# Attention by head pairs on halves of the TensorE array in steps of 512 queries, with projections, norms and weight folding rearranged in front of it

## What is computed

```python
x = x + attn_a(layernorm(x))          # binding by FFT, done as matmuls; not touched by the change
x = x + ffn(layernorm(x))             # top 2 of 8 low-rank experts
x = x + attn_b(layernorm(x))
x = x + ffn(layernorm(x))
# attn_b(x), with x already normalised once; 16 heads of 64
x_norm = (x - mu) / sqrt(var + 1e-5) * ln_w + ln_b        # a norm of the norm
q = l2norm(split_heads(x_norm @ Wq)); k = l2norm(split_heads(x_norm @ Wk))
v = split_heads(x @ Wv)
align = einsum('bhtd,bhsd->bhts', q, k)
resonance = sigmoid((align - 0.29514) * 15.0)
modulation = resonance * gate_q[..., :, None] * gate_k[..., None, :]   # q.gq and k.gk, by head
out = einsum('bhts,bhsd->bhtd', modulation, v) @ Wo + bo
```

## Time and profile before

| | |
|---|---|
| time, median of 3 runs | 2682.93 us (2682.44 to 2709.91) |
| time of the profiled execution | 2679.45 us |
| its span (slowest core, core 6) | 2677.8 us; the others 2663.7 to 2677.1 |
| PE, DVE, ACT, POOL busy | 56%, 41%, 25%, 1% of the span |
| granted TensorE clock, mean | 0.716 of full speed |
| lnC | 713 to 857 us |
| queries and keys, values, key norms | 857 to 1451 us |
| attention with Wo | 1451 to 2456 us |
| last ffn with its norm | 2456 to 2678 us |

### The profile page before, as it was taken

How to read it: one execution, slowest core, us unless ns; L and a number is a source line. 1 busy time by engine, 2 the same in 40 slices (tenths; PEclk the granted TensorE clock), 3 DMA queues, 4 the chain that set the end, 5 groups by cost and what they waited for, 6 DMA issues and landing times.

```text
span 2677.8 us, 18415 instructions; the slowest of 8 cores (2663.7 to 2677.8 us)
## 1 busy us (share of the span) xinstructions
PE 1488.9 (56%) x5855; PEld 567.4 (21%) x5930; DVE 1102.0 (41%) x1281; ACT 677.0 (25%) x677; POOL 35.7 (1%) x57
## 2 busy tenths in 40 slices
PE   1699966232111535358222888788767888875141
PEld 1234422120000212223000222222212222222110
DVE  5422231452366565643997332232233333212532
ACT  0000000000000000000221777776257777650000
POOL 1000000100000000000000000000000000001000
PEclk9999978655555767679555777777967777778555
DMA  7020114724411113210100000000210000007224
GB/s 157 32 32 24 48 55 169 161 64 140 158 63 63 47 55 71 63 32 16 32 0 0 0 1 0 1 0 1 91 35 1 0 1 0 1 1 164 95 81 170
DMA packets 63794, 142.27 MB, mean 53 GB/s; under 512 B 23507, under 2 KB 25043, under 8 KB 63702
## 3 DMA queue, kind: packets, MB, share of 16 engines
q1 hardware_dynamic: 36870, 124.28, 14.1%
q0 software_dynamic: 26832, 16.82, 4.9%
HBM read 119.10 MB, written 37.75 MB: 59 GB/s over the span
## 4 chain that ended last, share of the span: by engine, by line
PE 44%; DVE 19%; DMA 13%; ACT 10%; issue 7%; DVEq 6%; SPq 1%; ACTq 0%; POOLq 0%
DMA xcb<-xb 9%; ACT fmA L1128 8%; PE pP L704 7%; PE pP L652 6%; DMA xcb<-x 4%; PE pA L391 3%; PE pB L391 3%; PE pP L686 3%; PE pA L686 3%; DVEq L778 3%; PE pB L686 3%; PE pA L568 3%; DVE xcb L834 2%; PE pB L568 2%; PE pP L373 2%
## 5 line engine op out<-in xcount | busy, mean ns | idle before, releaser
L373 PE MATMUL pP<-ident,scb 128*128 128x128 bf16 x512 | 64.7, 306 | 390.2 <-DVE scb L805 251.6
L1128 ACT ACTIVATE fmA<-pA,cpool 128x1024 bf16<-128x1024 f32 x172 | 208.5, 1212 | 84.3 <-PE pA L686 84.3
L1128 ACT ACTIVATE fmA<-pP,cpool 128x1024 bf16<-128x1024 f32 x170 | 206.0, 1212 | 83.9 <-PE pP L686 78.8
L1128 ACT ACTIVATE fmA<-pB,cpool 128x1024 bf16<-128x1024 f32 x170 | 206.0, 1212 | 78.8 <-PE pB L686 78.7
L704 PE MATMUL pP<-fmA,act 128*64 128x512 bf16 x512 | 185.2, 541 | 0.0
L1053 DVE COPY handle<-pP 64x1024 f32<-64x1024 f32 x32 | 39.1, 1222 | 351.1 <-PE pP L704 351.1
L652 PE MATMUL pP<-fmA,act 128*64 128x512 bf16 x512 | 170.8, 507 | 5.6 <-ACT fmA L1128 5.6
L686 PE MATMUL pA<-act,act 64*128 64x512 bf16 x344 | 124.0, 447 | 49.5 <-ACT fmA L1128 42.5
L686 PE MATMUL pP<-act,act 64*128 64x512 bf16 x340 | 123.3, 449 | 49.0 <-ACT fmA L1128 42.1
L686 PE MATMUL pB<-act,act 64*128 64x512 bf16 x340 | 123.0, 448 | 47.8 <-ACT fmA L1128 40.9
L373 PEld LDWEIGHTS pP<-ident,scb 128*128 128x128 bf16 x512 | 49.5, 138 | 406.2 <-issue 406.2
(11 more groups left out here) (194 smaller groups left out, 1843.5 us busy)
## 6 DMA issues: line engine op xcount, KB each, us to landing
xcb<-xb SPq DMA_DIRECT2D x128, 512.0 KB, 3.9
xb<-xcb SPq DMA_DIRECT2D x48, 512.0 KB, 2.9
xcb<-x SPq DMA_DIRECT2D x32, 512.0 KB, 4.2
y<-xcb SPq DMA_DIRECT2D x16, 512.0 KB, 2.9
skew<-handle SPq DMA_DIRECT2D x16, 256.0 KB, 2.2
Wb<-aWk POOLq DMA_DIRECT2D x1, 2048.0 KB, 21.7
Wb<-aWv POOLq DMA_DIRECT2D x1, 2048.0 KB, 39.8
Wb<-aWq POOLq DMA_DIRECT2D x1, 2048.0 KB, 17.5
```

The source lines that it names most:

```text
L373: mm = t.transpose(pTb[:, base + 128 * j:base + 128 * (j + 1)], scb1[:, 128 * j:128 * (j + 1)], ident[:])
L1128: s.activation(RB[:, 1024 * sc:1024 * (sc + 1)], (pA, pB, pP1)[RING_SLOT[pos]][:], AF.Sigmoid, bias=cpool[:, 0:1], scale=cpool[:, 1:2]).th ...
```

## The change

- One-pass norm of the norm. The variance of a normed row follows from that of the row, so lnC computes both factors from one bn_aggr (swu, rwu), applies one scale and shift from x to the cast tile sqb, and evicts the transposes on ACT. fmA then holds x_norm (without ln_w and ln_b) for keys, queries and values alike, and the values are multiplied by cfac when they leave PSUM. The 32 repeated loads, norms and transposes are gone.
- ln_w is folded into Wk and Wq: SP loads them in f32 by 16 pieces into xcb, alternating with the loads of x, and POOL multiplies each piece into Wb1 or Wb0 and casts an unscaled copy (wub), of which PE makes the row ln_b @ W. That row goes through DRAM into a column (qkb) that ACT adds as a bias. Wv is loaded into act3 early, Wo into Wb1 after the keys.
- Projections by 16 units u (keys, then queries) of 128 outputs x 2048 tokens, in 4 chunks of 512. ACT writes keys or queries and their squares. PE sums the squares of a chunk over each head onto 32 columns of the array (norm_sums; the four chunks on four column groups of one PSUM bank); DVE clamps; POOL raises the sums to the power -0.5, splits the result into a bf16 high part and a rest, and PE spreads both from 32 rows of the array (norm_spread); DVE multiplies. Key gates come out token-major (gate_k), and POOL multiplies them into the values (v_scale).
- Attention by pairs of heads: 32 blocks b of 512 queries (half, pair, half of that), 16 steps each. In a step PE computes the scores of both heads, head a on rows 64a to 64a+63 of the array and into its own bank of pA or pB, and then the sums over the key tile of two steps ago, head a on columns 64a to 64a+63, both into one bank of pP1. ACT takes one sigmoid of 128 x 1024 (512 queries of two heads) into a ring of four places in xcb2. The score ring has two PSUM tensors instead of three.
- Wo of the first 1024 tokens is spread over the steps of the second half, 9 matmuls a block at most one in a step; that of the last 1024 stays behind the loop.
- At the start five more POOL instructions and two small loads stand ahead of the weight loads, and PE and DVE wait for POOL's whole setup before the first norm.

The diff, cut to its core:

```diff
+    colT = fmA
+    RB = AP(xcb2.ap().tensor, 0, [[2048, 128], [1, 2048]]).bitcast(BF16)
...
+        fence(g.memset(E4[:], 0.0))
...
+        g.dma_start(out=lnwc[:], in_=AP(dram["blnw"], 0, [[1, 128], [128, DC]]),
...
+        g.wait_ge(wf.lb, 16)
...
+        for i in range(16):
+            dc = i % DC
+            wst = xcb[:, 1024 * (i % 2):1024 * (i % 2) + 1024]
+            dst = Wb1 if i < DC else Wb0
+            g.wait_ge((wf.ld0, wf.ld1)[i % 2], 16 * (i // 2 + 1))
+            g.tensor_scalar(dst[:, 1024 * dc:1024 * (dc + 1)], wst,
+                            lnwc[:, dc:dc + 1], None, ALU.mult).then_inc(wf.fold, 1)
+            if i >= 2:
+                g.wait_ge(wf.mm, i - 1)
+            g.tensor_copy(wub[:, 1024 * (i % 2):1024 * (i % 2) + 1024], wst
+                          ).then_inc(wf.copy, 1)
...
+        def v_scale(u):
+            g.wait_ge(pr.ge, u + 1)
...
+            g.tensor_tensor(vv, vv, gb, ALU.mult).then_inc(pr.vs, 1)
...
+        for u in range(16):
+            if u == 8:
+                g.wait_ge(pr.pj, 32)
+                wload(Wb1, "bWo", wl.bWo)
+                bload("bbo", wl.bbo)
+            g.wait_ge(pr.cl, u + 1)
+            g.tensor_tensor(ssb[:], ssb[:], AP(mhalf.ap().tensor, 0, [[1, 128], [0, 512]]),
+                            ALU.pow)
+            g.drain()
+            g.tensor_copy(hib[:], ssb[:])
+            g.drain()
+            g.tensor_scalar(tmb[:], hib[:], nlo[:, 0:1], None, ALU.mult)
+            g.drain()
+            if u >= 1:
+                g.wait_ge(pr.bc, 4 * u)
+            else:
+                g.wait_ge(su.ee, 2)
+            g.tensor_tensor(hlb[:], ssb[:], tmb[:], ALU.add).then_inc(pr.rs, 1)
+            if 1 <= u <= 8:
+                v_scale(u - 1)
...
+                y.wait_ge(wf.fold, i - 1)
+                y.wait_ge(wf.copy, i - 1)
+            else:
+                y.wait_ge(ffB.ost0, 128)
+                y.wait_ge(ffB.ost1, 128)
+            y.dma_start(out=xcb[:, 1024 * (i % 2):1024 * (i % 2) + 1024],
+                        in_=AP(dram["bWk" if i < DC else "bWq"], 128 * 1024 * (i % DC),
+                               [[1024, 128], [1, 1024]])
+                        ).then_inc((wf.ld0, wf.ld1)[i % 2], 16)
+        for q in range(2):
...
-        ln_transposes(lnC, (ffB.te, TC), [])
...
+            t.wait_ge(wf.copy, tc + 1)
...
+        def proj(u, c):
+            ec = u % DC
+            W_ = Wb1 if u < DC else Wb0
+            if c == 0 and ec == 0:
+                t.wait_ge(wf.fold, 8 if u < DC else 16)
+            if u >= 1:
+                t.wait_ge(pr.sq, 4 * (u - 1) + c + 1)
+            else:
+                t.wait_ge(bv.ev, TC)
+            ps = psab(c // 2)[:, 512 * (c % 2):512 * (c % 2) + 512]
+            for dc in range(DC):
+                mm = t.matmul(ps, W_[:, 1024 * dc + 128 * ec:1024 * dc + 128 * (ec + 1)],
+                              fmA[:, T * dc + 512 * c:T * dc + 512 * (c + 1)],
+                              start=(dc == 0), stop=(dc == DC - 1))
+            mm.then_inc(pr.pj, 1)
...
+        def norm_sums(u):
+            t.wait_ge(pr.sq, 4 * u + 4)
+            if u >= 1:
+                t.wait_ge(pr.cl, u)
+            else:
+                t.wait_ge(wf.row, 2)
+            for c in range(4):
+                mm = t.matmul(pP1[32 * c:32 * c + 32, 0:512], E4[:, 0:32],
+                              sqb[:, 2048 * (u % 2) + 512 * c:
+                                  2048 * (u % 2) + 512 * (c + 1)],
+                              start=True, stop=True)
+            mm.then_inc(pr.ss, 1)
...
+        def norm_spread(u):
+            t.wait_ge(pr.rs, u + 1)
+            for c in range(4):
+                k = 4 * u + c
                 if k >= 2:
...
+                    t.wait_ge(pr.nm, k - 1)
                 else:
                     t.wait_ge(lnC.ev, TC)
...
+                    t.wait_ge(su.ee, 2)
+                t.matmul(pP2[:, 512 * (c % 2):512 * (c % 2) + 512],
+                         Ebc[32 * c:32 * c + 32, :], hlb[32 * c:32 * c + 32, :],
+                         start=True, stop=True).then_inc(pr.bc, 1)
...
+        def gate_k(u):
...
+            for tc in range(TC):
+                mm = t.matmul(pP1[:, 512 + 2 * tc:512 + 2 * tc + 2],
+                              act3[:, T * u + 128 * tc:T * u + 128 * (tc + 1)],
+                              gk2[:, 0:2], start=True, stop=True)
+            mm.then_inc(pr.gm, 1)
...
+        for u in range(18):
+            if u < 16:
+                proj(u, 0)
+            if 1 <= u <= 16:
+                norm_sums(u - 1)
+            if u < 16:
+                proj(u, 1)
+            if 2 <= u < 10:
+                gate_k(u - 2)
+            if u < 16:
+                proj(u, 2)
+                proj(u, 3)
+            if 1 <= u <= 16:
+                norm_spread(u - 1)
...
+        def scores(i):
+            b, sc = i // TC, i % TC
+            th, hp, tb = b // 16, (b // 2) % HP, b % 2
+            ps = psab(i)
+            q0 = T * hp + 1024 * th + 512 * tb
+            for a in range(2):
+                mm = t.matmul(ps[:, 512 * a:512 * (a + 1)],
+                              act3[64 * a:64 * a + 64,
+                                   T * hp + 128 * sc:T * hp + 128 * (sc + 1)],
+                              act2[64 * a:64 * a + 64, q0:q0 + 512],
                               start=True, stop=True)
...
+            mm.then_inc(at.al, 1)
...
+        def key_sums(i):
+            b, sc = i // TC, i % TC
+            hp = (b // 2) % HP
+            if sc == 0 and b >= 2:
+                t.wait_ge(at.ev, b - 1)
+            for a in range(2):
+                mm = t.matmul(pP1[64 * a:64 * a + 64, 512 * (b % 2):512 * (b % 2) + 512],
+                              act1[:, 1024 * sc + 128 * hp + 64 * a:
+                                   1024 * sc + 128 * hp + 64 * (a + 1)],
+                              RB[:, 1024 * (i % 4) + 512 * a:
+                                 1024 * (i % 4) + 512 * (a + 1)],
+                              start=(sc == 0), stop=(sc == TC - 1))
+            mm.then_inc(at.av, 1)
...
+        def gate_q(b):
+            th, hp, tb = b // 16, (b // 2) % HP, b % 2
+            if b >= 1:
+                t.wait_ge(at.ge, b)
+            q0 = T * hp + 1024 * th + 512 * tb
+            t.matmul(pP2[:, 512:1024], gq2rep[:], act2[:, q0:q0 + 512],
+                     start=True, stop=True).then_inc(at.gm, 1)
...
+        for i in range(32 * TC + 2):
+            if i >= 2:
+                t.wait_ge(at.sg, i - 1)
+            if i < 32 * TC:
+                scores(i)
+            if i == 2:
+                t.wait_ge(pr.vs, HP)
+                t.wait_ge(pr.ge, HP)
+            if i >= 2:
+                key_sums(i - 2)
+            if i % TC == 8:
+                gate_q(i // TC)
+            f, j = i // TC - 16, i % TC - 4
+            if 0 <= f < 16 and 0 <= j <= HP:
+                if j == 0:
+                    if f == 0:
...
-    RING_SLOT, RING_FREE = [], {}
...
+                mm = wo_mm(f, j, pP2[:, 0:512])
+                if j == HP:
+                    mm.then_inc(wo.mm, 1)
...
+            v.tensor_scalar(sqb[:, 2048 * (tc % 2):2048 * (tc % 2) + 1024],
+                            xcb2[:, 1024 * (tc % 2):1024 * (tc % 2) + 1024],
+                            mv1[:, 2 * tc:2 * tc + 1], rwu[:, 2 * tc:2 * tc + 1],
+                            ALU.subtract, ALU.mult).then_inc(lnC.app, 1)
...
+        for u in range(17):
+            if u < 16:
+                v.wait_ge(pr.ss, u + 1)
+                if u >= 1:
+                    v.wait_ge(pr.rs, u)
+                v.tensor_scalar(ssb[:], pP1[:, 0:512], 1e-24, None, ALU.max
+                                ).then_inc(pr.cl, 1)
+            if 1 <= u <= 8:
+                v.wait_ge(pr.gm, u)
+                if u >= 3:
+                    v.wait_ge(pr.vs, u - 2)
+                v.tensor_copy(gat[:, 32 * ((u - 1) % 2):32 * ((u - 1) % 2) + 32],
+                              pP1[:, 512:544]).then_inc(pr.ge, 1)
+            if u < 16:
+                dst = act3 if u < DC else act2
+                for c in range(4):
+                    o = T * (u % DC) + 512 * c
+                    v.wait_ge(pr.bc, 4 * u + c + 1)
+                    v.tensor_tensor(dst[:, o:o + 512], dst[:, o:o + 512],
+                                    pP2[:, 512 * (c % 2):512 * (c % 2) + 512],
+                                    ALU.mult).then_inc(pr.nm, 1)
...
+        for b in range(32):
+            th, hp, tb = b // 16, (b // 2) % HP, b % 2
+            o = T * hp + 1024 * th + 512 * tb
+            v.wait_ge(at.gm, b + 1)
+            v.tensor_copy(gqs[:], pP2[:, 512:1024]).then_inc(at.ge, 1)
+            if b >= 16:
+                wo_add(b - 16)
+            v.wait_ge(at.av, TC * (b + 1))
+            v.drain()
+            v.tensor_tensor(colT[:, o:o + 512], pP1[:, 512 * (b % 2):512 * (b % 2) + 512],
```

(17 more changed lines are left out.)

649 lines of the change are left out of this document (201 added, 448 removed).

## The result

The changed kernel takes 3180.21 us (median of 4 runs, 3159.76 to 3230.62); the kernel before took 2696.42 beside it (2682.44 to 2735.36). The ratio is 1.178, with a 95% interval from 1.166 to 1.191. In some executions the cores of one half of the chip show a lower clock and take some per cent longer, whatever the kernel; the medians and ranges in this text include those executions, the ratios do not. 2013 us were predicted. The profiled execution took 3164.59 us, its span is 3163.0.

What follows compares the result with a forecast made beforehand. PE and ACT wait for each other in turn in the attention; projections and norms take 594 us ahead. Attention -395, lnC -37, projections and norms -250, start +12: -670 on 2677.8 gives 2007.8, with 5.1 over the span 2013 us; range 1905 to 2205.

Steps and rivals of the forecast that it cites:

- the price at which the gain is gone: POOL's power in the units' loop: at 46 us each the gain of 670 us is eaten; slower-than-before rival, 50 us, 2754, chance 0.03.
- a price composed from other operations: POOL's power in the units' loop: 5.6 us each, from DVE's reciprocal and the two engines' products; three such give 16.8.

## What to carry to other kernels

When a change puts a function into a serial loop that no row of the trace shows on that engine, work out the price at which the gain is gone and ask what excludes it; a price composed from other operations excludes nothing, and one kernel that runs the function over a few sizes settles it. Cost every word of the diff, operands too: two constants in place of two columns were worth some 60 us in the old kernel by themselves. In a loop over several engines the latency of the chain sets the time, though no engine is full: with every link unchanged, its last one put a turn later gained 78 us of 1920.
